# A cross-attention stage whose second key projection, query transposes and one score mask change place

## The chip, the cores and the metric

The kernel runs on one core of a Trainium2 chip. The metric is the device time of one execution in microseconds (us). The five engines have one instruction queue each and meet through semaphores: TensorE (PE in the listings, its weight loads PEld), VectorE (DVE), ScalarE (ACT), GpSimd (POOL) and SyncE (SP), which here only issues DMAs.

## The reference

One decoder layer on x of shape (32, 112, 256) in float32: a gated delta-rule attention, a cross-attention to a context of 375 keys, and a mixture of six experts with a shared one. The change lies in the cross-attention, which is, for each of the 32 batch rows:

```python
Q = split(query @ wq.T); K = split(key @ wk.T); V = split(value @ wv.T)   # 16 heads of 16
scores = Q @ K.T / sqrt(16)
scores = where(mask == 1, -1e9, scores)
out = softmax(scores) @ V
x = x + out @ w_out.T
```

`query` is the layer norm of x; `key` and `value` are the context.

## The kernel before

The program has three stages. The delta attention takes the first 500 us, the cross-attention runs from about 500 to 1063 us, and the experts follow. Everything is scheduled by hand: each engine has its own `step` function, and the order of the calls in it is the order of its queue.

In the cross-attention a **step** works on batch row b. It has twelve **slots** q = 0 to 11. A slot is one third of the keys (125, on the partitions) by four heads of 112 queries: two score matmuls (L1147) into bank 0 or 1 of PSUM, by turns, then one exponential on ScalarE (L1653), and later sixteen matmuls with the values (L1161; they come four slots at a time, behind the scores of slots 1, 5 and 9). Masked keys get -2^40 before the scores are accumulated on top. For slots 2 to 9 ScalarE writes that mask into the bank (`write_mask`, L1662, once exponential q-2 has read the bank), and for the others TensorE makes it with a matmul of 448 columns (`mask_scores`, L1142).

Between the slots TensorE does work for other batch rows, by a fixed list:

- for the next row (b+1): the row maxima of the 16 heads. Each is one matmul of 376 columns (`row_max`, L1124) and one VectorE instruction (`maxima`, L2194). Three PSUM banks take turns, so that the matmul of head h waits for the VectorE result of head h-3. `MAXIMA` says how many heads are done at four places of each slot. Heads 5, 6 and 7 belong to slot 2, head 8 to slot 3, head 9 to slot 4, heads 10, 11 and 12 to slot 5.
- for the row after that (b+2): the key projection in two halves m = 0, 1 (`project_k`, six matmuls each, L875), which ScalarE rounds (`high_k`, L1628) and of which VectorE makes the low part (`low_k`, L2180); then two transposes of the normalised row (`transpose_h`, L1085), a copy on ScalarE (`copy_h`, L1632), the query projection (`project_q`, L1093), its rounding (`high_q`, L1636) and its low part (`low_q`, L2184). The second key half, the transposes and the queries share bank 7: `transpose_h` waits for `low_k` of both halves, and `project_q` waits for `copy_h`.
- for the row before (b-1): two transposes of the output heads (`transpose_on`, L1182), whose copy is `copy_on` (L1671), and the output projection (L1189).

SyncE spreads the rounded keys and queries over the score operands by DMA (`spread_keys`, then `spread_queries`, in this order in one queue). They are needed by `row_max` of the next step.

## Time and profile before

| | us |
|---|---|
| median of 3 runs (lowest, highest) | 1335.5 (1333.16, 1335.74) |
| the profiled execution's own time | 1333.69 |
| its span, first to last instruction | 1331.9 |
| TensorE busy over the span | 1223.9 (92%) |
| VectorE busy | 900.2 (68%) |
| ScalarE busy | 762.9 (57%) |
| GpSimd busy | 502.6 (38%) |

The span is divided among the stages as told above. Shares over the whole span are means over stages with different limits. What bounds the cross-attention is read from a stretch in its middle. TensorE's matmuls overlap, so that the distance from one start to the next, and not the duration, is what a matmul costs there.

### The profile page before, as it was taken

The numbers are of one execution on the slowest core, as the hardware profiler recorded it, in microseconds if no ns is written. First come the engines' busy times: TensorE is split into PE (matmuls) and PEld (weight loads), VectorE is DVE, ScalarE is ACT, GpSimd is POOL, SyncE is SP. The second block draws the span as 40 slices with busy tenths as digits, with TensorE's granted clock in tenths as the row PEclk, the third lists the DMA queues.
The fourth block names the chain that finished last, engine by engine and source line by source line (L and its number), as shares of the span: only waits on it lengthen the run. The fifth ranks groups of instructions, "written<-read, shape, count | busy, mean of one in ns | idle before, by whom it ended". The sixth has DMA issues, their size and how long they took to land.

```text
span 1331.9 us, 34415 instructions
## 1 busy us (share of the span) xinstructions
PE 1223.9 (92%) x10866; PEld 1105.3 (83%) x10866; DVE 900.2 (68%) x2932; ACT 762.9 (57%) x1780; POOL 502.6 (38%) x709
## 2 busy tenths in 40 slices
PE   4899999999998788999999999999999887999994
PEld 4789989889887777888888888889888776888884
DVE  4685674855846456778778877777887575655548
ACT  3543344343343317788888888888888853555530
POOL 2242241322321332344444444444444451333335
PEclk9999999999999888899999999999999898999997
DMA  8499800000000235465666665556566143333358
GB/s 205 113 221 227 188 0 0 0 0 0 0 0 23 67 97 123 126 153 142 151 150 149 152 149 145 142 141 155 141 158 153 47 142 89 104 101 101 105 141 246
DMA packets 131263, 151.39 MB, mean 114 GB/s; under 512 B 41107, under 2 KB 111108, under 8 KB 131156
## 3 DMA queue, kind: packets, MB, share of 16 engines
q1 hardware_dynamic: 124436, 134.55, 42.1%
q0 software_dynamic: 6160, 15.69, 3.5%
q8 instruction: 42, 0.69, 0.2%
q14 instruction: 49, 0.40, 0.1%
q10 hardware_dynamic: 576, 0.07, 0.0%
HBM read 79.27 MB, written 45.82 MB: 94 GB/s over the span
## 4 chain that ended last, share of the span: by engine, by line
PE 47%; ACT 5%; DVE 4%; issue 3%; DMA 2%; POOL 2%; SPq 1%; ACTq 0%; DVEq 0%; POOLq 0%
PE psum L875 8%; PE psum L1161 6%; PE psum L1147 6%; PE psum L1124 6%; PE psum L1296 6%; PE psum L1316 3%; ACT pr L1653 2%; PE psum L1142 2%; PE psum L1093 2%; PE psum L1189 2%; ACT psum L1662 1%; PE psum L1339 1%; PE psum L1208 1%; DVE x_res L2331 1%; PE psum L1287 1%
## 5 line engine op out<-in xcount | busy, mean ns | idle before, releaser
L2194 DVE CUSTOM_DVE_ANT_0 junk<-psum,biasq 112x375 f32<-112x375 f32 x512 | 267.0, 541 | 102.1 <-issue 66.1
L1653 ACT ACTIVATE pr<-psum 125x448 f32<-125x448 f32 x384 | 203.7, 539 | 29.6 <-PE psum L1147 27.9
L1147 PE MATMUL psum<-qst,kst 97*125 97x224 f32 x768 | 198.0, 318 | 10.5 <-ACT psum L1662 10.0
L1124 PE MATMUL psum<-kst,qst 96*112 96x376 f32 x512 | 167.7, 354 | 3.0 <-DVE smax L2194 2.9
L1147 PEld LDWEIGHTS psum<-qst,kst 97*125 97x125 f32 x768 | 141.6, 192 | 27.3 <-ACT psum L1662 26.2
L1662 ACT ACTIVATE psum<-flagk 125x448 f32<-125x448 bf16 x256 | 140.7, 550 | 7.6
L717 POOL TENSOR_TENSOR rs<-rs,neg_half 112x1 f32<-112x1 f32 x32 | 18.2, 570 | 248.7 <-DVE rs L2107 248.7
L841 POOL DMA_INDIRECT routed_y<-yb,yrow x61 | 58.8, 964 | 123.5 <-ACT yb L1841 120.9
L1124 PEld LDWEIGHTS psum<-kst,qst 96*112 96x112 f32 x512 | 90.2, 181 | 11.1 <-DVE smax L2194 8.2
L1161 PE MATMUL psum<-pr,vaug 125*32 125x112 f32 x3072 | 96.6, 268 | 0.0
L759 POOL DMA_INDIRECT routed_h<-h,slot x64 | 78.2, 1223 | 32.4 <-POOL h L748 14.7
L1161 PEld LDWEIGHTS psum<-pr,vaug 125*32 125x32 f32 x3072 | 72.6, 112 | 14.6 <-issue 5.9
L1571 ACT COPY xq<-psum 112x224 f32<-112x224 f32 x80 | 27.1, 348 | 85.1 <-PE psum L983 83.2
L2426 DVE TENSOR_TENSOR hidb<-sgb,psum 128x256 f32<-128x256 f32 x61 | 25.7, 421 | 62.6 <-ACT sgb L1826 62.5
L668 POOL TENSOR_TENSOR cT<-negT,masks_sb 112x448 f32<-112x448 f32 x48 | 61.3, 1305 | 6.5 <-DVE negT L1967 6.5
L1518 ACT CAST hidhi<-hid 128x448 fp32r<-128x448 f32 x32 | 18.1, 566 | 75.5 <-DVE hid L1942 75.5
L983 PE MATMUL psum<-tri,cT 112*112 112x112 f32 x320 | 41.2, 270 | 19.3 <-DVE triT L1972 10.8
L983 PEld LDWEIGHTS psum<-tri,cT 112*112 112x112 f32 x320 | 37.1, 182 | 23.3 <-POOL cT L668 13.3
L1826 ACT ACTIVATE sgb<-psum 128x256 f32<-128x256 f32 x61 | 23.4, 384 | 56.8 <-PE psum L1296 56.8
L712 POOL TENSOR_SCALAR biasq<-maskq 112x375 f32<-112x375 int32 x32 | 49.9, 1560 | 10.3 <-DMA maskk<-in_maskT 5.4
L996 PE MATMUL psum<-xq,triT 112*112 112x112 f32 x320 | 48.2, 274 | 3.7 <-ACT xq L1571 3.2
L1142 PE MATMUL psum<-flagk,negbig 125*125 125x448 bf16 x128 | 47.8, 373 | 0.9 <-DMA qst<-negm 0.9
(320 smaller groups left out, 3525.0 us busy)
## 6 DMA issues: line engine op xcount, KB each, us to landing
kst<-khi SPq DMA_DIRECT2D x64, 376.0 KB, 4.5
routed_h<-in_route_pad SPq DMA_DIRECT2D x6, 3640.0 KB
kst<-klo SPq DMA_DIRECT2D x32, 376.0 KB, 6.1
ctxT<-in_ctxT SPq DMA_DIRECT2D x32, 375.0 KB, 3.5
hblk<-routed_h SPq DMA_DIRECT2D x61, 130.0 KB, 2.1
qst<-qhi SPq DMA_DIRECT2D x128, 56.0 KB, 2.4
stage<-in_e SPq DMA_DIRECT2D x21, 256.0 KB, 3.4
maskq<-in_mask SPq DMA_DIRECT2D x32, 164.1 KB
```

The source lines that it names most:

```text
L668: nc.gpsimd.tensor_tensor(cT[:, n], negT[:], over_rows(M_BT + 1 + n), op=ALU.mult).then_inc(s["cmask"], 1)
L759: pool.indirect_dma_start(hbuf[:, :], to, h3[par][:], None).then_inc(s3["scat"], 16)
L875: mm = pe.matmul(to, st, mv, start=n == 0, stop=n == len(products) - 1)
L983: mm = pe.matmul(bank[6 + u][0:T, cols(j % 2)], cT[:, n, j], tri[:, j], start=True, stop=True)
L1124: pe.matmul(bank[max_bank(n, par, hd)][0:T, 0:S2E], head(qst[par][0:ROWS], hd), pair(kst[par][0:ROWS], hd // 2), start=True, stop=True).th ...
L1142: pe.matmul(bank[q % 2][0:KP, 0:GT], negbig[:], flags, start=True, stop=False, skip_group_check=True)
L1147: mm = pe.matmul(bank[q % 2][0:KP, cols(i, 2 * T)], pair(kst[par], n)[:, cols(q // HPB, KP)], both(qst[par], n), start=False, stop=True, s ...
L1161: mm = pe.matmul(bank[6][row:row + 2 * HD, cols(hd // HPB)], vaug[par][:, c3, hd], pr[q % PROBS][:, i], start=q == 0, stop=c3 == KC - 1, s ...
L1296: mm = pe.matmul(bank[4 + u][0:BLK, :], hp, e13[wp][:, bass.ds(e, 1), c].rearrange("p a w n -> p (a w n)"), start=n == 0, stop=n == len(pa ...
L1653: nc.scalar.activation(pr[q % PROBS][:].rearrange("k i q -> k (i q)"), bank[q % 2][0:KP, 0:GT], ACT.Exp, scale=1.0 / HD ** 0.5).then_inc(s ...
L1662: nc.scalar.activation(bank[q % 2][0:KP, 0:GT].rearrange("k (i q) -> k i q", i=HPB), flags, ACT.Copy, scale=-BIG).then_inc(s["cmask"], 1)
L2194: nc.vector.tensor_tensor_reduce(out=junk[:, hd % 2, :], in0=bank[max_bank(n, par, hd)][0:T, 0:S2], in1=biasq[:, par, :], scale=1.0, scala ...
```

## The change

In TensorE's `step`, the second half of the key projection goes from slot 2 to slot 3, in front of the transposes of the row before. The transposes of h go from before the values of slot 5 to behind them, and the transposes of the output heads go ahead of the query projection. ScalarE's list follows: rounding of the second key half in slot 3, mask of slot 7 ahead of the copy of h, and the mask of slot 10 is written by ScalarE too, between the negated maxima and the copy of the values. VectorE makes the second low part of the keys at the head of slot 5, where it was at the head of slot 3.

```diff
-WRITTEN = range(2, 10)
+WRITTEN = range(2, 11)
...
                     if q in WRITTEN:
-                    pe.wait_ge(s["cmask"], G * len(LEVELS) + len(WRITTEN) * b + q - WRITTEN[0] + 1)
+                    pe.wait_ge(s["cmask"], G * len(LEVELS) + len(WRITTEN) * b + WRITTEN.index(q) + 1)
...
-                    if q == 5 and following >= 2:
-                        transpose_h(*far)
                     if q % HPB == 1 and q > HPB:
                         for earlier in range(q - HPB - 1, q - 1):
                             weighted_values(t, par, earlier)
...
+                    if q == 5 and following >= 2:
+                        transpose_h(*far)
                     if q == 1 and early >= 2:
                         route(*ahead(t, par, -2))
                     if maxima:
                         row_max(*nxt, heads_at(q, 2))
-                    if q in (1, 2) and following >= 2 and not first:
-                        project_k(*far, q - 1)
+                    if q in (1, 3) and following >= 2 and not first:
+                        project_k(*far, q // 2)
                     if q == 3 and not first:
                         transpose_o(*prev)
+                    if q == 5 and not first:
+                        transpose_on(*prev)
                     if q == 5 and following >= 2:
                         project_q(*far)
-                    if q == 5 and not first:
-                        transpose_on(*prev)
...
                     exponentials(t, par, q)
+                    if q + 2 in WRITTEN and q < 8:
+                        write_mask(t, par, q + 2)
                     if q == 5 and following >= 2:
                         copy_h(*far)
-                    if q + 2 in WRITTEN:
-                        write_mask(t, par, q + 2)
                     if q == 1 and not first:
                         copy_pv(*prev)
-                    if q in (1, 2) and following >= 2:
-                        high_k(*far, q - 1)
+                    if q in (1, 3) and following >= 2:
+                        high_k(*far, q // 2)
...
                     if q == 8 and following >= 1:
                         negate_max(*nxt)
+                    if q == 8:
+                        write_mask(t, par, 10)
...
-                        if place == 0 and q == 3 and following >= 2:
+                        if place == 0 and q == 5 and following >= 2:
                             low_k(*far, 1)
```

What the change moves, as the queues of the two programs list it.

TensorE, slots 2 and 3 before: scores and heads 5 and 6, then the second key half (the three L875 lines), head 7, and slot 3 with head 8, and the four transposes of the row before (L1175):

```order
L1147 MATMUL psum<-qst,kst 125x224
L1124 MATMUL psum<-kst,qst 112x376
L875 MATMUL psum<-chi,wxk_hi 128x376 x2
L875 MATMUL psum<-clo,wxk_hi 128x376 x2
L875 MATMUL psum<-chi,wxk_lo 128x376 x2
L1124 MATMUL psum<-kst,qst 112x376
L1147 MATMUL psum<-qst,kst 125x224 x2
L1124 MATMUL psum<-kst,qst 112x376
L1175 MATMUL psum<-ident_sb,pv 112x128 x4
```

And with the change:

```order
L1147 MATMUL psum<-qst,kst 125x224
L1124 MATMUL psum<-kst,qst 112x376 x2
L1147 MATMUL psum<-qst,kst 125x224 x2
L1124 MATMUL psum<-kst,qst 112x376
L875 MATMUL psum<-chi,wxk_hi 128x376 x2
L875 MATMUL psum<-clo,wxk_hi 128x376 x2
L875 MATMUL psum<-chi,wxk_lo 128x376 x2
L1175 MATMUL psum<-ident_sb,pv 112x128 x4
```

Heads 6 and 7, slot 3 and head 8 now follow each other without the projection between them.

TensorE, the end of slot 5 before: heads 10 and 11 around a score matmul, the transposes of h, sixteen value matmuls, head 12, the queries, the transposes of the output heads:

```order
L1124 MATMUL psum<-kst,qst 112x376
L1147 MATMUL psum<-qst,kst 125x224
L1124 MATMUL psum<-kst,qst 112x376
L1085 MATMUL psum<-ident_sb,h 128x112 x2
L1161 MATMUL psum<-pr,vaug 32x112 x16
L1124 MATMUL psum<-kst,qst 112x376
L1093 MATMUL psum<-h2T,xwq_sb 128x112 x4
L1182 MATMUL psum<-ident_sb,on 128x112 x2
```

And with the change:

```order
L1124 MATMUL psum<-kst,qst 112x376
L1147 MATMUL psum<-qst,kst 125x224
L1124 MATMUL psum<-kst,qst 112x376
L1161 MATMUL psum<-pr,vaug 32x112 x16
L1085 MATMUL psum<-ident_sb,h 128x112 x2
L1124 MATMUL psum<-kst,qst 112x376
L1182 MATMUL psum<-ident_sb,on 128x112 x2
L1093 MATMUL psum<-h2T,xwq_sb 128x112 x4
```

Between the transposes of h and the queries stood the values and a head; now a head and two transposes stand there.

ScalarE, slots 2 to 5 before: after exponential 2 come mask 4, the second rounding of the keys (L1628), exponential 3, mask 5, the router's small exponential (L1682), exponential 4, mask 6, exponential 5, the copy of h (L1632), mask 7:

```order
L1662 ACTIVATE psum<-flagk 125x448 [waits c_exp]
L1628 CAST khi<-psum 128x376 [waits c_k_ps]
L1653 ACTIVATE pr<-psum 125x448 [waits c_pv_done,c_sc_ps]
L1662 ACTIVATE psum<-flagk 125x448 [waits c_exp]
L1682 ACTIVATE prob<-logit 112x6 [waits e_prob]
L1653 ACTIVATE pr<-psum 125x448 [waits c_pv_done,c_sc_ps]
L1662 ACTIVATE psum<-flagk 125x448 [waits c_exp]
L1653 ACTIVATE pr<-psum 125x448 [waits c_pv_done,c_sc_ps]
L1632 COPY h2T<-psum 128x224 [waits c_hT_ps]
L1662 ACTIVATE psum<-flagk 125x448 [waits c_exp]
L1636 CAST qhi<-psum 128x224 [waits c_q_ps]
```

And with the change:

```order
L1662 ACTIVATE psum<-flagk 125x448 [waits c_exp]
L1653 ACTIVATE pr<-psum 125x448 [waits c_pv_done,c_sc_ps]
L1662 ACTIVATE psum<-flagk 125x448 [waits c_exp]
L1628 CAST khi<-psum 128x376 [waits c_k_ps]
L1682 ACTIVATE prob<-logit 112x6 [waits e_prob]
L1653 ACTIVATE pr<-psum 125x448 [waits c_pv_done,c_sc_ps]
L1662 ACTIVATE psum<-flagk 125x448 [waits c_exp]
L1653 ACTIVATE pr<-psum 125x448 [waits c_pv_done,c_sc_ps]
L1662 ACTIVATE psum<-flagk 125x448 [waits c_exp]
L1632 COPY h2T<-psum 128x224 [waits c_hT_ps]
L1636 CAST qhi<-psum 128x224 [waits c_q_ps]
```

Mask 5 no longer stands behind a rounding of the keys, and the copy of h stands behind mask 7.

## Rows read from the trace of the kernel before

**Rows 1.** Busy time in a stretch of the cross-attention: us, engines, clock, DMA, GB/s.

```profile
700.00:800.00 100.00, 99.03 (x1135) 89.27 (x1134) 80.49 (x336) 82.29 (x186) 45.71 (x79) 1.00 0.62 150
```

**Rows 2.** Waits, 600 to 1000 us (23 batch rows): total us, times, longest.

```profile
PEld psum L1147 <- ACT psum L1662: 13.9, 46, 0.4
```

**Rows 3.** Timeline of TensorE, slots 2 to 5: start us, us, engine, line, operation.

```profile
773.03 0.33 PE L1124 MATMUL psum<-kst,qst 96*112 96x376 f32 x1
...
773.48 0.51 PE L875 MATMUL psum<-chi,wxk_hi 128*128 128x376 f32 x2
...
774.68 0.38 PE L1147 MATMUL psum<-qst,kst 97*125 97x224 f32 x2
...
774.89 0.34 PE L1124 MATMUL psum<-kst,qst 96*112 96x376 f32 x1
...
775.84 0.27 PE L1147 MATMUL psum<-qst,kst 97*125 97x224 f32 x1
...
776.27 0.18 PEld L1147 LDWEIGHTS psum<-qst,kst 97*125 97x125 f32 x1 [0.41 <-ACT psum L1662]
...
776.76 0.34 PE L1124 MATMUL psum<-kst,qst 96*112 96x376 f32 x1
```

**Rows 4.** Timeline of TensorE, slots 8, 10 and 11 of the same batch row.

```profile
781.23 0.48 PE L1147 MATMUL psum<-qst,kst 97*125 97x224 f32 x2
781.55 0.41 PE L875 MATMUL psum<-wxv_hi,chi 128*125 128x256 f32 x2
...
785.15 0.40 PE L1142 MATMUL psum<-flagk,negbig 125*125 125x448 bf16 x1
...
785.61 0.35 PE L1142 MATMUL psum<-flagk,negbig 125*125 125x448 bf16 x1
...
786.01 0.51 PE L1124 MATMUL psum<-kst,qst 96*112 96x376 f32 x2
```

**Rows 5.** Timeline of ScalarE: copy of the values behind slot 8.

```profile
783.43 0.59 ACT L1641 COPY vaug<-psum 125x512 f32<-125x512 f32 x1 [0.61 <-PE psum L875]
```

**Rows 6.** Timeline of VectorE: head 5, second low part, head 9, sigmoid sum.

```profile
773.53 0.55 DVE L2194 CUSTOM_DVE_ANT_0 junk<-psum,biasq 112x375 f32<-112x375 f32 x1 [0.68 <-issue]
...
775.49 0.54 DVE L2180 TENSOR_TENSOR klo<-psum,khi 128x376 fp32r<-128x376 f32 x1
...
776.41 0.54 DVE L2194 CUSTOM_DVE_ANT_0 junk<-psum,biasq 112x375 f32<-112x375 f32 x1
...
777.51 0.16 DVE L2122 TENSOR_SCALAR prob<-prob 112x6 f32<-112x6 f32 x1
```

**Rows 7.** Timeline of TensorE, from the values of slot 5 to slot 6.

```profile
777.22 0.97 PE L1161 MATMUL psum<-pr,vaug 125*32 125x112 f32 x32
778.12 0.43 PE L1124 MATMUL psum<-kst,qst 96*112 96x376 f32 x1
778.39 1.04 PE L1093 MATMUL psum<-h2T,xwq_sb 128*128 128x112 f32 x8
779.26 0.36 PE L1182 MATMUL psum<-ident_sb,on 112*128 112x112 f32 x2
```

**Rows 8.** Timeline of ScalarE: exponential 4, copy of h, mask 7, queries, exponential 6.

```profile
776.25 0.53 ACT L1653 ACTIVATE pr<-psum 125x448 f32<-125x448 f32 x1
...
777.71 0.34 ACT L1632 COPY h2T<-psum 128x224 f32<-128x224 f32 x1
777.94 0.56 ACT L1662 ACTIVATE psum<-flagk 125x448 f32<-125x448 bf16 x1
779.47 0.35 ACT L1636 CAST qhi<-psum 128x224 fp32r<-128x224 f32 x1 [0.97 <-PE psum L1093]
...
780.06 0.55 ACT L1653 ACTIVATE pr<-psum 125x448 f32<-125x448 f32 x1
```

**Rows 9.** Key spread in SyncE's timeline; its DMA issues on the page (us to landing).

```profile
776.49 0.61 SPq L493 DMA_DIRECT2D kst<-klo  x1
...
kst<-klo SPq DMA_DIRECT2D x32, 376.0 KB, 6.1
```

## The prediction

> **What bounds the kernel now.** I read the busy times of a stretch in the middle of the cross-attention first. TensorE is busy in 99.03 of 100 us at a granted clock of 1.00, which is 2.4 GHz, while VectorE is at 80 and ScalarE at 82 [rows 1]. So a batch row costs what TensorE's queue costs, its waits included. The list of waits comes next, to see which of them are TensorE's own. The scores wait for masks that ScalarE writes: 13.9 us in 46 waits over 23 batch rows, two in each [rows 2]. The timeline of one batch row then shows where. I use the row that runs through slot 2 at 773 us and slot 11 at 786 us. One wait stands at slot 5, where TensorE is idle for 0.41 us before a score [rows 3]; the other is at slot 8 and small. The change touches what stands ahead of slot 5, and one mask matmul. 29 of the 32 batch rows (1 to 29) get all of it, and the rest of the program nothing, so the sum is made for one row and taken 29 times.
>
> **The mask of slot 10.** Before, slot 10 lasts from 785.15 to 785.61, 0.46 us, with its mask matmul, and it starts after a wait. Slot 8 starts after a wait too and has no mask matmul; it lasts from 781.23 to 781.55, 0.32. The difference is 0.14 us [rows 4]. In a slot that follows without a gap it is more: slot 11 takes 0.40 [rows 4], slot 3 without a mask takes 0.21 [rows 3], so 0.19. After a wait the first score's weights load in the open, which the mask matmul hid. I take 0.14, since slot 10 follows the values and a gap; the ends are 0 and 0.19. "TensorE: Matmul & The Clock Gate" of the Trainium skill, section "Back-to-back issue gap", gives columns / 2.4 GHz plus 2.5 ns, which is 189 ns for 448 columns, and by it the sum would be 0.05 us a row smaller; the slots without a gap agree with it, slot 10 does not have its conditions. ScalarE pays a mask write of some 0.55 us more. It stands where ScalarE is idle for 0.61 us, in front of the copy of the values [rows 5], so I cost it at nothing; without that cover the copy and exponential 9 would come later, and slot 11's mask with them.
>
> **The wait at slot 5.** Mask 5 now follows exponential 3 directly, and exponential 3 comes earlier because slot 3's scores do not stand behind the projection. The 0.41 goes.
>
> **What is late next: head 8.** The projection and head 7 are seven matmuls of 376 columns between 773.48 and 774.68, so the six of the projection are 1.03 us. Without them in front, head 8 is reached at 774.89 - 1.03 = 773.86 [rows 3]. It needs the maximum of head 5, which shares its bank. TensorE starts head 5 at 773.03 [rows 3], and VectorE starts on it at 773.53, after having waited for it, for 0.55 us, to 774.08 [rows 6]. With 0.05 for the signal (TensorE's queries end at 778.39 + 1.04 = 779.43 and ScalarE starts on them at 779.47 [rows 7, 8]) TensorE goes on at 774.13: a new wait of 0.27, and 0.09 for the open weight load, which I read from head 12 after the values, 778.12 to 778.39 instead of 0.17 [rows 7]. Queued behind it are the whole projection, the transposes of the row before and slot 4. So of the 0.41 gained 0.36 is given back, and head 11 comes at 776.71 where it was at 776.76 [rows 3].
>
> **What is late after that: the transposes of h.** The values follow head 11 after 0.17 + 0.09, at 776.97, and last 0.90 [rows 7], so TensorE reaches the transposes at 777.87. Two things hold them and the queries behind them:
>
> - VectorE. The transposes overwrite the second key half, whose low part is now made in slot 5. Head 9 stands 0.17 before the score at 775.84 [rows 3] and comes 0.36 later, at 776.03; VectorE starts on it 0.50 after that, as with head 5, at 776.53. From there to the sigmoid sum it needs 1.10 (776.41 to 777.51) and then the low part begins, at about 777.70, and takes 0.54 [rows 6]. With the signal the transposes start at 778.29, a wait of 0.42. They end some 0.42 later (two of this size take 0.36 [rows 7], and the first weights load in the open), and ScalarE has them at 778.75.
> - ScalarE. Exponential 4 was at 776.25 [rows 8]; it now needs slot 4's scores, which end at 775.84 + 0.36 + 0.27 [rows 3], so it comes at 776.51. The copy of h was 1.46 behind it [rows 8]. Now mask 7 is in between, 0.56 [rows 8] and about 0.1 until exponential 5 has ended. The copy could start at 778.63.
>
> The later of the two decides: copy of h at 778.75, 0.34 long [rows 8], queries at 779.14 where they were at 778.39 [rows 7]. That is 0.75 later. The transposes of the output heads stand in this gap now instead of behind the queries, which gives 0.13 back to TensorE, so its slot 6 is 0.62 later. But ScalarE then has the rounding of the queries and the copy of the output heads directly in front of exponential 6. The rounding comes at about 780.23 (0.76 later), each copy holds ScalarE for 0.23 to 0.24 (777.71 to 777.94), and exponential 6 starts at 780.71 instead of 780.06 [rows 8]. Mask 8 follows it and slot 8 waits for mask 8, as today [rows 2]. So slot 8 comes 0.65 later.
>
> **Queues.** SyncE issues the keys' spreads later: the rounding of the second half moves by about 1.1 us and its low part from 775.49 to 777.70. The last of them was issued at 776.49 and lands after 6.1 us [rows 9], at 782.6; 2.2 later is 784.8. The next row's first heads need it at 786.01 [rows 4], so this is hidden. The queries' spreads move with their rounding, 0.65 to 0.76, and the heads that need them by 0.51; that slack shrinks by some 0.2 and no wait on a DMA appears in the list for them. GpSimd is not touched.
>
> **The sum.** +0.65 at slot 8, -0.14 at slot 10, so +0.51 us a row; everything behind slot 10 follows TensorE and shifts with it. Times 29 it is 14.8 us. Rows 0, 30 and 31 bring under half a microsecond. The profiled execution's span of 1331.9 becomes 1346.7 and its time of 1333.7 becomes 1348.5; the median of the runs lies 1.8 above it, so I forecast **1350**. For the ends: if head 8 and the low part held TensorE not at all, exponential 4 would stay at 776.25, the copy of h would start at 778.37 and the queries at 778.76, 0.37 late, of which 0.27 reach slot 8; net +0.13 a row, +4 us. If each of four handovers costs 0.05 more and the mask matmul gives nothing, it is +0.85 a row, +25 us.
>
> **The rivals.**
> - *Faster.* The place is the start of the query projection. If VectorE finishes the low part and ScalarE the copy of h before TensorE has done the values, head 12 and the transposes of the output heads, nothing is given back: -0.41 - 0.14 = -0.55 a row, 16 us, 1319.5. It decides at the queries' start: at 777.98 in this row's time all is gained, at 778.39 nothing but the mask. For it speaks that both engines are idle for a fifth of the time [rows 1]; against it, that both queues are full exactly here, with mask 7 put ahead of the copy. 18 in 100, partial gains included.
> - *No change.* The new waits eat just the 0.55. The queries would start at about 778.6. 7 in 100.
> - *A little slower.* The VectorE waits are absent and only mask 7 delays the copy: +4 us, 1339.5. 12 in 100.
> - *The clock falls.* The granted clock is 1.00 here while TensorE is 99% busy [rows 1]; the change puts two or three gaps of 0.3 to 0.4 us in each batch row. Each microsecond at 1.2 GHz loses half a microsecond: a tenth of the stage's 500 us would cost 25 on top of the 15, 1375. The same page of the Trainium skill, section "A second HAM failure mode: psum-queue depth-cycling", tells of a kernel whose short idles between groups made the clock go to and fro; here, gaps of 0.41 in each row have not done it. 3 in 100.
> - That the change doesn't do what it says is not open: the queues in the listing have the new order, and the mask matmuls fall from four to three a row.
>
> **How the numbers follow.** My forecast has 60 in 100; with the two other slower cases it is 75 for slower. A measurement of this kernel can tell about 0.2%, 2.7 us, from no change. The range goes from 1333, which takes in no change and the little loss, to 1361, the upper bound of the waits. It leaves out the faster rival and the clock, about 2 in 10.
>
> **What would show it.** The mask wait before slot 5 should be gone from the waits, and mask matmuls fall from 128 to 96. New lines should be TensorE waiting for VectorE's maxima at L1124 (0.27 a row), for the low part at the transposes of h (0.42) and for the copy of h at the queries, and the copy of h should stand 0.9 to 1.1 us later against slot 2. A batch row should last 0.51 us more. I am wrong if TensorE does not wait between the values of slot 5 and the queries, or if slot 8 comes no later against slot 2.

## The result, and the profile after

| | before | changed |
|---|---|---|
| median, 4 runs each (lowest to highest), us | 1334.35 (1333.16 to 1335.74) | 1348.36 (1346.43 to 1350.19) |
| the profiled execution's own time | 1333.69 | 1348.22 |
| its span | 1331.9 | 1346.1 |
| one batch row of the cross-attention, median | 17.48 | 18.10 |

The ratio of the changed kernel to the one before is 1.0104, 95% interval 1.0085 to 1.0124: slower by 1%, as forecast (1350). A batch row is measured here and below from one negation of the maxima (L1647, once a row) to the next, in the middle of the stage; the forecast for it was +0.51 us and it is +0.62.

The first reading is the same as before: busy times of 100 us of the changed kernel in the middle of the stage (length, then PE, PEld, DVE, ACT, POOL, then granted clock, DMA share, GB/s).

```profile
707.00:807.00 100.00, 96.65 (x1076) 85.67 (x1074) 77.21 (x323) 81.99 (x183) 43.80 (x78) 1.00 0.60 146
```

TensorE was busy for 99.03 of 100 us [rows 1] and now is for 96.65; VectorE fell as well, and ScalarE stayed although it got a mask more a row. No engine has become the bound. The same queue has holes in it. The list of waits of the changed kernel, 600 to 1000 us (22 or 23 batch rows; who waits <- for whom: total us, times, longest), says which. It is read at the weight loads (PEld), whose idle time at such a wait is longer than the matmuls' (0.62 and 0.38 us at L1085, below):

```profile
PEld psum L1085 <- DVE klo L2182: 13.6, 22, 0.6
...
PEld psum L1124 <- DVE smax L2196: 6.9, 23, 0.3
PEld psum L1147 <- ACT psum L1662: 6.5, 22, 0.3
...
PEld psum L1093 <- ACT h2T L1632: 6.1, 22, 0.3
```

One wait in each row for the second low part, one for a maximum, one for the copy of h, and of the two waits for a mask [rows 2] one is left. 13.9 us in all have gone down to 6.5, and 26.6 us (13.6, 6.9 and 6.1) have come. The timeline of the weight loads of one batch row places them (start, duration; in brackets the idle time before it and what ended it):

```profile
781.17 0.17 PEld L1124 LDWEIGHTS psum<-kst,qst 96*112 96x112 f32 x1 [0.30 <-DVE smax L2196]
...
785.31 0.20 PEld L1085 LDWEIGHTS psum<-ident_sb,h 112*128 112x128 f32 x2 [0.62 <-DVE klo L2182]
786.15 0.97 PEld L1093 LDWEIGHTS psum<-h2T,xwq_sb 128*128 128x128 f32 x8 [0.28 <-ACT h2T L1632]
789.01 0.29 PEld L1147 LDWEIGHTS psum<-qst,kst 97*125 97x125 f32 x2 [0.29 <-ACT psum L1662]
```

To set this row beside the one of [rows 3 to 8], take 7.03 off its times: the first score of slot 2 starts at 772.92 there and at 779.95 here. A time with 7.03 taken off is called "in the old row" below. TensorE of the changed kernel, the places that [rows 3, 4, 7] show of before:

```profile
781.17 0.42 PE L1124 MATMUL psum<-kst,qst 96*112 96x376 f32 x1
...
783.69 0.33 PE L1124 MATMUL psum<-kst,qst 96*112 96x376 f32 x1
783.96 0.97 PE L1161 MATMUL psum<-pr,vaug 125*32 125x112 f32 x32
785.31 0.41 PE L1085 MATMUL psum<-ident_sb,h 112*128 112x112 f32 x2 [0.38 <-DVE klo L2182]
...
785.74 0.36 PE L1182 MATMUL psum<-ident_sb,on 112*128 112x112 f32 x2
786.16 1.15 PE L1093 MATMUL psum<-h2T,xwq_sb 128*128 128x112 f32 x8
787.07 0.35 PE L1147 MATMUL psum<-qst,kst 97*125 97x224 f32 x1
...
789.01 0.48 PE L1147 MATMUL psum<-qst,kst 97*125 97x224 f32 x2
...
792.95 0.48 PE L1147 MATMUL psum<-qst,kst 97*125 97x224 f32 x2
793.26 0.35 PE L1142 MATMUL psum<-flagk,negbig 125*125 125x448 bf16 x1
```

Head 8 starts at 781.17, 774.14 in the old row; the transposes of h at 778.28 and the queries at 779.13, where they were at 778.39. Slot 8 starts at 781.98 instead of 781.23, 0.75 late. Slot 10 has no mask matmul any more and lasts 0.31 (792.95 to 793.26) instead of 0.46 [rows 4]. ScalarE and VectorE of the same row, at the handovers that feed these waits:

```profile
783.51 0.55 ACT L1653 ACTIVATE pr<-psum 125x448 f32<-125x448 f32 x1 [0.16 <-PE psum L1147]
...
785.12 0.55 ACT L1662 ACTIVATE psum<-flagk 125x448 f32<-125x448 bf16 x1
785.76 0.35 ACT L1632 COPY h2T<-psum 128x224 f32<-128x224 f32 x1
787.34 0.35 ACT L1636 CAST qhi<-psum 128x224 fp32r<-128x224 f32 x1 [1.23 <-PE psum L1093]
...
787.82 0.56 ACT L1653 ACTIVATE pr<-psum 125x448 f32<-125x448 f32 x1
...
790.50 0.54 ACT L1662 ACTIVATE psum<-flagk 125x448 f32<-125x448 bf16 x1
791.22 0.59 ACT L1641 COPY vaug<-psum 125x512 f32<-125x512 f32 x1 [0.18 <-PE psum L875]
```

```profile
784.64 0.16 DVE L2124 TENSOR_SCALAR prob<-prob 112x6 f32<-112x6 f32 x1
784.71 0.54 DVE L2182 TENSOR_TENSOR klo<-psum,khi 128x376 fp32r<-128x376 f32 x1
```

The low part runs from 784.71 to 785.25 and TensorE goes on at 785.31. The weight loads stood idle for 0.62 us there, but part of that lay under the values' matmuls, which take 0.90 us as before [rows 7] and so keep TensorE until about 784.86: the queue loses some 0.45 us (predicted 0.42). The copy of h starts at 785.76, 0.09 behind the end of mask 7 (785.67) and right after the transposes. Mask 10, at 790.50, uses the idle time of [rows 5]: the copy of the values behind it still waits 0.18 us for TensorE.

### The profile page after: what moved, and what is told of

Same layout as the page of the kernel before. It is cut to its first block, busy times and chain, and to the rows that moved or that the text cites. A ratio compares the mean times of both kernels' runs of the same rounds, so it can differ in the third digit from the quotient of the medians.

```text
span 1346.1 us, 34407 instructions
## 1 busy us (share of the span) xinstructions
PE 1228.0 (91%) x10834; PEld 1101.4 (82%) x10834; DVE 898.9 (67%) x2932; ACT 783.0 (58%) x1812; POOL 502.3 (37%) x709
## 4 chain that ended last, share of the span: by engine, by line
PE 41%; DVE 8%; issue 7%; ACT 3%; DMA 2%; SPq 1%; POOL 1%; DVEq 0%; POOLq 0%; ACTq 0%
PE psum L875 8%; PE psum L1296 5%; PE psum L1147 5%; PE psum L1124 4%; PE psum L1161 4%; PE psum L1316 3%; PE psum L1093 3%; DVE junk L2196 2%; PE psum L1189 2%; PE psum L1142 1%; PE psum L1208 1%; DVE klo L2182 1%; PE psum L1085 1%; DVE x_res L2333 1%; PE psum L1287 1%
## 5 line engine op out<-in xcount | busy, mean ns | idle before, releaser
L1147 PE MATMUL psum<-qst,kst 97*125 97x224 f32 x768 | 187.7, 310 | 6.5 <-ACT psum L1662 6.4
L1124 PE MATMUL psum<-kst,qst 96*112 96x376 f32 x512 | 164.8, 356 | 7.3 <-DVE smax L2196 2.9
L1662 ACT ACTIVATE psum<-flagk 125x448 f32<-125x448 bf16 x288 | 157.6, 547 | 8.6
L1147 PEld LDWEIGHTS psum<-qst,kst 97*125 97x125 f32 x768 | 137.9, 191 | 24.2 <-ACT psum L1662 17.9
L1124 PEld LDWEIGHTS psum<-kst,qst 96*112 96x112 f32 x512 | 87.6, 180 | 16.6 <-DVE smax L2196 14.4
L1161 PEld LDWEIGHTS psum<-pr,vaug 125*32 125x32 f32 x3072 | 72.1, 111 | 15.7 <-issue 11.2
L1000 PE MATMUL psum<-triT,xq 112*112 112x112 f32 x320 | 47.8, 276 | 0.0
```

The source lines that it names most:

```text
L1124: pe.matmul(bank[max_bank(n, par, hd)][0:T, 0:S2E], head(qst[par][0:ROWS], hd), pair(kst[par][0:ROWS], hd // 2), start=True, stop=True).th ...
L1147: mm = pe.matmul(bank[q % 2][0:KP, cols(i, 2 * T)], pair(kst[par], n)[:, cols(q // HPB, KP)], both(qst[par], n), start=False, stop=True, s ...
L1161: mm = pe.matmul(bank[6][row:row + 2 * HD, cols(hd // HPB)], vaug[par][:, c3, hd], pr[q % PROBS][:, i], start=q == 0, stop=c3 == KC - 1, s ...
L1662: nc.scalar.activation(bank[q % 2][0:KP, 0:GT].rearrange("k (i q) -> k i q", i=HPB), flags, ACT.Copy, scale=-BIG).then_inc(s["cmask"], 1)
```

## The experiments

The theory is that of the prediction: the mask brings 0.14 us a row, and the moves cost 0.65 (by the result 0.76) because the chain VectorE's low part, transposes, copy, queries, rounding, exponential 6, mask 8 now stands in TensorE's way. The rivals: the mask write is what costs; the transposes' new place costs and the keys' does not; or the sum is of another make than the terms. There are twelve runs, four on each of three chips; three of the last four repeat an earlier kernel. On the second and third chip every traced kernel has a disturbance that the first does not show (last section), so rows of those kernels are medians over the undisturbed rows. The kernel before was traced once, so every row is set beside that trace.

**1. The mask alone.** Before, with the mask of slot 10 written by ScalarE:

```diff
-WRITTEN = range(2, 10)
+WRITTEN = range(2, 11)
...
-                    if q + 2 in WRITTEN:
+                    if q + 2 in WRITTEN and q < 8:
...
+                    if q == 8:
+                        write_mask(t, par, 10)
```

> The kernel before with only the mask of slot 10 written by ScalarE (between the negated maxima and the copy of the values). Theory: slot 10 follows a wait, so its first weight load comes into the open and the mask matmul was worth 0.14 us a row, in 32 rows 4.5 us: the time falls to about 1330. Rival A: the whole 0.19 us of a mask matmul is gained, 6 us. Rival B: the mask write delays the copy of the values and exponential 9, and nothing is gained.

Measured: 1328.49 against 1333.91, ratio 0.9975 (0.9957 to 0.9994). The row is 17.33, 0.14 shorter. That is the value taken for a slot behind a gap, and not the 0.19 of the slots without one. The mask write costs nothing that shows, so that rival falls, and this part of the change shortens the row by itself. (The time on a third chip, below, does not show the gain.)

**2. Only the keys moved.** Before, with the second key projection, its rounding and its low part in their new places, and nothing else:

```diff
-                    if q in (1, 2) and following >= 2 and not first:
-                        project_k(*far, q - 1)
+                    if q in (1, 3) and following >= 2 and not first:
+                        project_k(*far, q // 2)
...
-                    if q in (1, 2) and following >= 2:
-                        high_k(*far, q - 1)
+                    if q in (1, 3) and following >= 2:
+                        high_k(*far, q // 2)
...
-                        if place == 0 and q == 3 and following >= 2:
+                        if place == 0 and q == 5 and following >= 2:
```

> The kernel before with only the second key projection moved (TensorE slot 3, rounding in slot 3, low part at the head of slot 5), the transposes of h still ahead of the values. Theory (VectorE's low part holds the transposes): TensorE reaches them at slot 5's end and waits 1.4 us for the low part; the wait before slot 5 is gone and head 8 waits 0.3; about +1.35 us a row, +39 us. Rival (ScalarE's mask 7 ahead of the copy is what costs): here the copy has its old place, so the kernel should be near the one before or faster by the 0.41 of slot 5.

Measured: 1368.77, ratio 1.0267 (1.0242 to 1.0291); the row is 18.87, 1.40 longer. Its waits, 600 to 1000 us:

```profile
PEld psum L1085 <- DVE klo L2180: 32.3, 21, 1.5
...
PEld psum L1124 <- DVE smax L2194: 6.6, 22, 0.3
PEld psum L1147 <- ACT psum L1662: 4.2, 21, 0.2
```

The transposes of h, still in front of the values of slot 5, stand 1.5 us before the low part: more than twice the wait of the changed kernel, where the 0.90 us of the values lie between. The wait at slot 5 has gone here too. So the keys' move alone is the dearest part of the change, and the transposes' move repairs about half of it: with both, and the mask's 0.14 left out, the row is 0.76 longer instead of 1.40.

**3. Only the transposes moved.** Before, with the transposes of h behind the values, those of the output heads ahead of the queries, and mask 7 ahead of the copy of h:

```diff
-                    if q == 5 and following >= 2:
-                        transpose_h(*far)
                     if q % HPB == 1 and q > HPB:
...
+                    if q == 5 and following >= 2:
+                        transpose_h(*far)
...
-                    if q == 5 and following >= 2:
-                        project_q(*far)
                     if q == 5 and not first:
                         transpose_on(*prev)
+                    if q == 5 and following >= 2:
+                        project_q(*far)
...
-                    if q == 5 and following >= 2:
-                        copy_h(*far)
                     if q + 2 in WRITTEN:
                         write_mask(t, par, q + 2)
+                    if q == 5 and following >= 2:
+                        copy_h(*far)
```

> The kernel before with only the moves around the values of slot 5 (transposes of h behind them, those of the output heads ahead of the queries, mask 7 ahead of the copy of h); the key projection stays in slot 2. Theory: the copy of h can start only when transposes (778.35 in the frame of the batch row told of) and mask 7 (778.36) allow, the queries come 0.39 later, and slot 8 about 0.40 later: +12 us, with no wait for the low part and the 0.41 before slot 5 still there. Rival (only VectorE's lateness costs): no change.

Measured: 1345.01, ratio 1.0084 (1.0064 to 1.0105), row 17.89, 0.41 longer. Its waits:

```profile
PEld psum L1147 <- ACT psum L1662: 15.7, 45, 0.4
PEld psum L1093 <- ACT h2T L1632: 6.1, 22, 0.3
```

The mask waits of before stay and the wait for the copy of h comes, without VectorE in it. The three parts give -0.14, +1.40 and +0.41, together +1.67 where the change costs +0.62. They do not add: each shifts the moment at which the next handover is due. That is why one chain has to be followed, and not parts added.

**4. The changed kernel with the copy of h ahead of mask 7 again.** If mask 7 were the reason for the late copy, this would give time back.

```diff
-                    if q + 2 in WRITTEN and q < 8:
-                        write_mask(t, par, q + 2)
                     if q == 5 and following >= 2:
                         copy_h(*far)
+                    if q + 2 in WRITTEN and q < 8:
+                        write_mask(t, par, q + 2)
```

> The changed kernel with the copy of h again ahead of mask 7 on ScalarE. Theory: the transposes end later than mask 7 allows (copy at 785.76, ScalarE free at about 785.60), so the order of the two makes no difference: within 1 us of the changed kernel. Rival (mask 7 in front is the cause): 0.4 us a row back, -12 us against the changed kernel.

Measured: 1348.79, ratio 1.0119 (1.0091 to 1.0148); row 18.08, the same as the changed kernel within 0.02. With the low part as late as it is, ScalarE's order does not count.

**5. The changed kernel with the low part ahead of head 9** (slot 4 instead of slot 5 in VectorE's list; second chip, as 6 to 8, where before took 1341.57):

```diff
-                        if place == 0 and q == 5 and following >= 2:
+                        if place == 0 and q == 4 and following >= 2:
```

> The changed kernel with VectorE's second low part of the keys ahead of head 9 (head of slot 4) instead of at the head of slot 5. Theory: the transposes no longer wait (0.45 us earlier), but the copy of h then stands behind mask 7, which frees ScalarE only 0.16 earlier than today: -0.16 us a row, -5 us against the changed kernel. Rival (VectorE alone is the cause): -0.45 a row, -13 us.

Measured: 1353.28, ratio to before 1.0077 (1.0053 to 1.01). The row is 17.92, 0.17 less than with the change. Its waits:

```profile
PEld psum L1093 <- ACT h2T L1632: 12.4, 22, 0.6
```

The wait of 0.6 for the low part is gone and most of it has come back one step later, where 0.3 for the copy of h has become 0.6. Now mask 7 decides, which the prediction had 0.12 us earlier than the low part's chain.

**6. Both: the low part ahead of head 9 and the copy of h ahead of mask 7** (the edits of 4 and 5):

```diff
-                    if q + 2 in WRITTEN and q < 8:
-                        write_mask(t, par, q + 2)
                     if q == 5 and following >= 2:
                         copy_h(*far)
+                    if q + 2 in WRITTEN and q < 8:
+                        write_mask(t, par, q + 2)
...
-                        if place == 0 and q == 5 and following >= 2:
+                        if place == 0 and q == 4 and following >= 2:
```

> As the one with the early low part, and the copy of h ahead of mask 7 too. Theory: both holders of the copy are taken away together: queries 0.45 us earlier, -13 us against the changed kernel, about the time of the kernel before. Rival: no more than the one with the early low part.

Measured: 1345.52, ratio 1.003 (1.0012 to 1.0049), row 17.64, 0.46 less. The edit that brought 0.01 alone now brings 0.28. Two engines held TensorE at one place, one behind the other; only taking both away shows the price of either.

**7. The changed kernel with head 8 behind the key projection,** so that the projection does not queue behind the wait for the maximum:

```diff
-                        if maxima:
+                        if maxima and (q, i) != (3, 1):
                             row_max(*nxt, heads_at(q, i))
...
+                    if maxima and q == 3:
+                        row_max(*nxt, heads_at(3, 1))
```

> The changed kernel with head 8's matmul behind the second key projection instead of ahead of it (TensorE only). Theory: its wait of 0.27 plus 0.09 is in the chain of everything behind it, since head 9 and slot 4 come earlier and with them VectorE's low part and ScalarE's exponential 4: -0.36 us a row, -10 us against the changed kernel. Rival (the later waits swallow it): no change.

Measured: 1348.22, ratio 1.0048 (1.003 to 1.0065), row 17.76, 0.34 less. So the second wait that the prediction named is as dear as it said (0.36), and it is passed on in full, although the low part is still late: the projection, its rounding and the low part stand behind head 8 too.

**8. All three** (the edits of 6 and 7 together).

```diff
-                        if maxima:
+                        if maxima and (q, i) != (3, 1):
                             row_max(*nxt, heads_at(q, i))
...
+                    if maxima and q == 3:
+                        row_max(*nxt, heads_at(3, 1))
...
+                    if q == 5 and following >= 2:
+                        copy_h(*far)
                     if q + 2 in WRITTEN and q < 8:
                         write_mask(t, par, q + 2)
-                    if q == 5 and following >= 2:
-                        copy_h(*far)
...
-                        if place == 0 and q == 5 and following >= 2:
+                        if place == 0 and q == 4 and following >= 2:
```

> The changed kernel with all three: low part ahead of head 9, copy of h ahead of mask 7, head 8 behind the key projection. Theory: the queries start 0.86 us earlier than in the changed kernel, 0.1 earlier than in the one before, and the mask of slot 10 is gained: 0.25 us a row against the kernel before, about 1328. Rival: the two fixes overlap and it only gets back to the kernel before.

Measured: 1334.32, ratio 0.9945 (0.9927 to 0.9964). The row is 17.33: 0.76 less than with the change and 0.14 less than before. I had expected 0.86 and 0.25, so a tenth of a us is missing. Its time, 1334.32 against 1341.57, gains more than the 4 us that 29 such rows make; the experiments on the third chip come back to that. Its waits show where:

```profile
PEld psum L1147 <- ACT psum L1664: 7.1, 24, 0.3
...
PEld psum L1093 <- ACT h2T L1634: 5.9, 23, 0.3
```

The queries still wait 0.26 us a row for the copy of h, with no engine late in front of it. In the row at 811 us ScalarE stands idle for 0.18 us before the transposes release it, copies from 815.71 to 816.06, and TensorE goes on at 816.11, 0.85 us after it started the transposes (815.26). One head and the transposes of the output heads are too short to cover that. The 0.76 that the change lost are back, to a hundredth; the 0.41 at slot 5 are no gain beyond the mask even so.

**9 to 12. Side by side, on a third chip** (before 1343.33 there, 1335.74 to 1348.27): the mask alone again, all three again, a new mixture, and the changed kernel again. The mixture is before with the mask of slot 10, the keys' move with its low part ahead of head 9, and head 8 behind it; the transposes of h, the queries and mask 7 stay where they were. Not repeated below are the mask's edit, which is that of experiment 1, and the rounding's, which is that of experiment 2:

```diff
-                        if maxima:
+                        if maxima and (q, i) != (3, 1):
                             row_max(*nxt, heads_at(q, i))
...
-                    if q in (1, 2) and following >= 2 and not first:
-                        project_k(*far, q - 1)
+                    if q in (1, 3) and following >= 2 and not first:
+                        project_k(*far, q // 2)
+                    if maxima and q == 3:
+                        row_max(*nxt, heads_at(3, 1))
...
-                        if place == 0 and q == 3 and following >= 2:
+                        if place == 0 and q == 4 and following >= 2:
```

> The same kernel as e1_mask10 (before, with only the mask of slot 10 written by ScalarE), now beside the next three on one chip. Theory (the mask is worth 0.14 us a batch row wherever the rest stands): 0.9970 of before, 4 us faster, row -0.14. Rival (its first interval, 0.9957 to 0.9994, was near 1, and it is nothing): 1.000.

> The same kernel as e8_all (changed, with the low part ahead of head 9, the copy of h ahead of mask 7, head 8 behind the key projection). Theory: a row of -0.13 us against before as in its first run, ratio 0.9945 to 0.9970, so about the same as the mask alone: the moves give back what they take, no more. Rival (the moves bring something of their own once the waits are gone): 2 us or more faster than the mask alone, 0.9945 or lower.

> Before, with the mask of slot 10 by ScalarE, the second key projection in slot 3 with head 8 behind it, and its low part ahead of head 9 of slot 4; the transposes of h stay in front of the values of slot 5 and mask 7 behind the copy of h. Theory: the 0.41 us wait at slot 5 goes, but the low part, which VectorE starts at the end of head 7's or 8's maximum, about 776.3 in the time of the row of before, ends at 776.8, when TensorE would reach the transposes of h at 776.7 or earlier; a wait of 0.1 to 0.4 is left there, and the row is -0.14 to -0.35 against before: ratio 0.993 to 0.997. Rival (the low part still comes a microsecond late, as in e2_keys_only): row +0.2 or more, ratio 1.004 or more.

> The changed kernel again, as the measure on this chip: ratio 1.0085 to 1.0124 as in its first runs, row +0.62 us against before.

| | median | ratio to before (95%) | undisturbed row |
|---|---|---|---|
| mask alone | 1342.30 | 0.9997 (0.9982 to 1.0012) | 17.34 |
| all three | 1337.42 | 0.9959 (0.994 to 0.9977) | 17.33 |
| the mixture | 1336.42 | 0.9953 (0.9939 to 0.9966) | 17.31 |
| the changed kernel | 1355.88 | 1.0102 (1.0085 to 1.0119) | 18.09 |

The changed kernel's loss is the same on this chip. In undisturbed rows the first three are alike, to 0.03 us; by that the mask is all there is to gain. In time they are not: the mask alone, 0.25% faster on the first chip, shows nothing here, and the other two are 5 to 6 us faster than it. My expectation of its time was wrong, while its row is as expected. Of the rival of the second, the first half holds (more than 2 us faster than the mask alone) and the second does not (a ratio of 0.9945 or lower; it is 0.9959).

Two things outside the undisturbed rows point at the difference. One is the disturbance of the last section: between 600 and 1000 us seven rows are longer, by 1.33 us each with the mask alone, by 1.06 with all three and 0.95 in the mixture. The other is the clock in the third batch row (last section): that step took 21.9 us with the mask alone and 18.7 in both others. From the first to the last negation of the maxima the mask alone takes 562.6 us, all three 556.5 and the mixture 553.6; the two things make 5.1 and 5.9 us of the 6.1 and 9.0 between them. The runs point the same way for the clock: over 12 runs each, the mean granted clock of an execution is 0.9676 with the mask alone and 0.9701 with all three. A stretch at half clock takes half its share of the span off the mean and costs half its length, so that is 3.3 us by estimate (0.0025 of 1337), with a difference of only twice its standard error. But the traces do not prove the explanation: the profiled execution of all three gave its 6 us back outside the cross-attention, where the kernels are the same, and its span is that of the mask alone (1338.8 and 1338.9).

In the mixture the low part ends 0.3 us late for the transposes of h, as expected:

```profile
PEld psum L1085 <- DVE klo L2184: 6.8, 22, 0.4
...
PEld psum L1147 <- ACT psum L1664: 4.6, 23, 0.2
```

It is 0.47% faster than the kernel before, on that chip. It is not told apart from all three, which had 0.9959 beside it and 0.9945 in experiment 8 (the intervals overlap); these two are the best found.

## Why the prediction was right

Each step in the old row's time, in us, from the timelines shown above:

| step | predicted | measured |
|---|---|---|
| head 8 starts | 774.13 | 774.14 |
| exponential 4 | 776.51 | 776.48 |
| head 11 | 776.71 | 776.66 |
| low part starts | 777.70 | 777.68 |
| transposes of h start | 778.29 | 778.28 |
| copy of h | 778.75 | 778.73 |
| queries start | 779.14 | 779.13 |
| rounding of the queries | 780.23 | 780.31 |
| exponential 6 | 780.71 | 780.79 |
| slot 8 later by | 0.65 | 0.75 |
| slot 10 shorter by | 0.14 | 0.15, 0.14 in experiment 1 |
| a batch row | +0.51 | +0.62 |

- **The wait at slot 5** went, and the wait for head 5's maximum came in its place (0.30 on the weight load, 0.27 predicted). Experiment 7 shows its price, 0.34 (predicted 0.36).
- **The low part and mask 7** both hold the copy of h, the low part last. Experiments 4 to 6 show exactly this: mask 7 alone nothing, the low part alone 0.17, both 0.46.
- **The mask of slot 10** brought what a slot behind a gap gives. The Trainium skill, "TensorE: Matmul & The Clock Gate", section "Back-to-back issue gap", gives columns / 2.4 GHz plus 2.5 ns as the gap of a single matmul at full clock, which is 189 ns for 448 columns. The slots without a wait in front agree with it (0.19); slot 10 has a wait in front, and the row of experiment 1 says 0.14. The two scores of slot 10 now last 0.48 instead of the 0.38 of two scores in [rows 3], which fits a weight load that the mask matmul had covered and that is now in the open.
- **The term that was mis-sized** is the step from the queries to exponential 6 in "ScalarE then has the rounding of the queries and the copy of the output heads directly in front of exponential 6". The rounding was put 0.76 later, as far as the queries themselves (0.75), so the eight query matmuls were taken to last 1.04 as in [rows 7]. They last 1.15 here, since their first weight load now follows a wait: the 0.09 that I charged to head 8 for the same reason, and not to them. All kernels bear this out. Between 600 and 1000 us the eight matmuls take 1.14 to 1.15 us a row in every kernel in which they wait for the copy of h (the changed kernel, experiments 3 to 8), and 1.04 to 1.05 in those in which they do not (before, the mask alone, the keys alone, the mixture). This made exponential 6 0.08 and slot 8 0.10 later than said, and that is 0.10 of the 0.11 which the row has more.
- **The queues.** The keys' spreads stayed hidden. For the queries' spreads I said that no wait appears. In the middle none does, but in two rows, between 571.6 and 609.1 us, heads waited for the low part of the queries, and these rows took 18.66 and 18.84 us instead of 18.10. SyncE's issue of such a spread had taken 1.63 us in the first, where an issue of a low part takes 0.61 in [rows 9]:

```profile
571.47 1.63 SPq L501 DMA_DIRECT2D qst<-qlo  x1
```

```profile
PE psum L1124 <- DMA qst<-qlo: 0.8, 2, 0.5
```

  This is not the change's doing alone: the mask alone has such waits in both its traces, in which no spread was moved, and the second trace of the changed kernel (experiment 12) has none. How far the move of the spreads adds to it is not shown.

- **The total** is nearer than its make deserves. 29 rows of 0.62 are 18.0 us, and the span grew by 14.2. From the first to the last negation of the maxima the kernel before takes 552.7 us (489.9 to 1042.6) and the changed one 569.1 (489.7 to 1058.8), 16.4 more; behind the last one 289.3 and 287.3, 2.0 less, in a part that the change does not touch and where the half-clock stretches of one execution fall differently from another's. Of the 16.4, the two late rows are 1.3. The third row gives back the rest: it took 21.9 before and 19.5 now, where its neighbours grew. The busy times of that row, first before and then changed, show the granted clock in the third column from the right:

```profile
533.40:555.30 21.90, 19.88 (x195) 17.85 (x194) 16.55 (x52) 15.08 (x34) 7.32 (x7) 0.84 0.41 102
```

```profile
534.10:553.60 19.50, 17.07 (x194) 14.84 (x193) 16.27 (x50) 15.51 (x36) 7.99 (x7) 1.00 0.46 117
```

TensorE was at 1.2 GHz for 6.8 of those us before, and not at all in the changed kernel. I had counted this row at +0.51 like the others; it came out at -2.5, which is 3.1 us off the +0.62 of the rest. That the total fits so well is luck in part: without this row's clock it would be 17 us instead of 14. The forecast also put the median of the runs 1.8 above the profiled execution; over four runs each it is 0.7 above it before and 0.1 with the change, and that alone takes 1.7 off the forecast of 1350.

**The rivals.** The faster one fell because TensorE's weight loads stood at the transposes for 0.62 us before the low part let them go, and at the queries for 0.28 more. "No change" needed the queries at 778.6; they came at 779.13. "A little slower" needed VectorE to be on time, which experiment 5 had to bring about by an edit, and even then the row was 0.44 longer than before and not 0.13, since head 8 kept its wait. The clock did not fall: it is 1.00 from 560 to 1040 us, with holes of 0.3 to 0.6 us in every row.

## What to carry to other kernels

When one queue is the bound and a wait in it is removed by moving work, the work is late wherever it is consumed: write down for the moved piece when its last consumer is reached, and follow the chain through every engine up to the next place where the bounding queue joins it, open weight loads after a wait included (some 0.1 us each here). When two engines hold the same place, undoing either shows a part of the price or none; undo both before calling one harmless. And look for a part of a change that stands by itself: here the mask alone shortens every row by 0.14 us (0.25% of the time on one chip, nothing measurable on another), while the moves cost five times as much.

## What I had not expected of the hardware

**The clock of one batch row differs between the kernels.** The profiled executions of the kernel before and of the mask alone (both times) show a half-clock stretch near 540 us, of 3.4 to 6.8 us. None of the other executions shows one there, with the keys or the transposes moved. In front of it TensorE was busy for 3.2 of 5 us, in both kernels (535 to 540 us; before, then changed), with one wait of 1.8 us on VectorE's h at L1197 (the line below each, idle time in brackets):

```profile
535.00:540.00 5.00, 3.20 (x39) 2.50 (x29) 5.00 (x7) 3.23 (x8) 3.86 (x4) 1.00 0.29 78
```

```profile
538.49 0.41 PE L1197 MATMUL psum<-ident_sb,h 112*128 112x112 f32 x2 [1.80 <-DVE h L2112]
```

```profile
535.00:540.00 5.00, 3.22 (x49) 2.62 (x48) 5.00 (x5) 3.69 (x9) 3.80 (x4) 1.00 0.30 81
```

```profile
539.01 0.41 PE L1197 MATMUL psum<-ident_sb,h 112*128 112x112 f32 x2 [1.78 <-DVE h L2114]
```

So the idle time is the same and only one of the two loses its clock. Nor does the length of that wait tell them apart: it is 1.96 and 1.97 us with the mask alone, which lose the clock like the kernel before with 1.80, but 1.87 in the mixture, which keeps it. What decides it stays open, and with one trace of most kernels it is not shown that the order of the work does. It is worth 2 to 3 us, beside a mask whose whole gain is 4.

**On two of the three chips VectorE and ScalarE stand still once in three rows.** On the first chip no row of any kernel has it. On the others about one row in three is longer in all eight traces, by 0.84 to 1.33 us in the mean, and the median of the kernel before is 1341.57 and 1343.33 there instead of 1334. The runs of a chip were taken together, so the chip is not told apart from the hour. The rows of the mask alone on the third chip show it, first VectorE, then ScalarE, then TensorE (idle time and its releaser in brackets; "issue" is a wait for nothing that the profile shows, "remote" a release by something that it does not name):

```profile
725.91 0.55 DVE L2196 CUSTOM_DVE_ANT_0 junk<-psum,biasq 112x375 f32<-112x375 f32 x1 [1.97 <-issue]
```

```profile
725.68 0.53 ACT L1667 COPY pv<-psum 128x448 f32<-128x448 f32 x1 [1.33 <-remote]
```

```profile
726.60 0.61 PE L875 MATMUL psum<-chi,wxk_hi 128*128 128x376 f32 x2 [0.95 <-DVE logit L2119]
```

VectorE's pause always sits at the same instruction, 8.5 to 9.0 us behind the negated maxima; in the other rows it starts that instruction after 0.3 us. ScalarE's copy of the sums over the values (L1667) is held in most of these rows too: it starts about 8.5 us behind the negated maxima instead of 7.0, and here 0.23 us before VectorE. Between 600 and 1000 us only the traces of the second and third chip have such waits (6 to 8 each, 6.3 to 11.2 us in all). So it is not VectorE alone that stands still. By the program both instructions wait for results of TensorE, whose matmuls in this row run on until 725.65. VectorE's idle time then runs into a wait of TensorE, and how much of it TensorE feels differs with the order of work, 0.84 to 1.33 us a row. With the mask alone it is the key projection that waits (10.1 us in 8 waits), with all three a head (L1124, 9.2 us in 9). That is one way in which an order of work with the same undisturbed row can come out faster. What stops the two engines was not found, and no run here tells it.
